# Mixing product of a two-layer kernel: from full-array products to two 64-row halves of the array

## What is computed

```python
x = x + _L0_ffn_ref(_L0_cond_ref(x, ...), L0_ffn_weight)      # grouped convolution, then an int8-style product
x = x + _L1_ffn_ref(_L1_cond_ref(x, ...), W, b, A, Bmat, LiMEs)

# _L1_cond_ref: every batch b has its own 64 x 64 weight, built from 8 kernels
agg_w = jnp.einsum('bk,koi->boi', att, weight[..., 0])
out = jnp.einsum('boi,bih->boh', agg_w, x) + agg_b[:, :, None]
```

## Time and profile before

| | before |
|---|---|
| median of 3 executions | 752.04 us (751.64 to 752.83) |
| profiled execution | 748.49 us |
| its span, first to last instruction | 746.6 us |
| mean granted TensorE clock | 0.995 |
| PE / PEld / DVE / ACT / POOL busy | 729.5 / 436.6 / 413.5 / 285.8 / 275.3 us |
| mixing product: PE busy, records | 64.1 us, 512 |
| mixing product: PEld busy, records | 59.7 us, 512 |

### The profile page before, as it was taken

One profiled execution on the slowest core, in us unless ns is written; L12 is line 12 of the kernel. 1 busy time (PEld: TensorE's weight loads), 2 busy tenths in 40 slices (PEclk: granted clock), 3 DMA queues, 4 the chain that ended last, 5 costly groups with the idle time before them and its releaser, 6 DMA issues. The chain is left out here.

```text
span 746.6 us, 10961 instructions
## 1 busy us (share of the span) xinstructions
PE 729.5 (98%) x3966; PEld 436.6 (58%) x3998; DVE 413.5 (55%) x863; ACT 285.8 (38%) x540; POOL 275.3 (37%) x158
## 2 busy tenths in 40 slices
PE   7989999999999999999999999999999999999998
PEld 6666676777777777767755444444444444444443
DVE  5756777777777877777855486523132222222233
ACT  2656887746656655555552223310111011001000
POOL 3012213213677632221245418964443443343000
PEclk9899999999999999999999999999999999999999
DMA  9579675675776565455236104533434343342102
GB/s 318 193 102 368 249 260 195 223 252 189 239 243 231 205 225 202 174 191 198 85 113 255 57 29 169 220 148 140 169 120 157 146 160 123 146 164 85 57 29 112
DMA packets 47766, 129.58 MB, mean 174 GB/s; under 512 B 16402, under 2 KB 16786, under 8 KB 47538
## 3 DMA queue, kind: packets, MB, share of 16 engines
q1 hardware_dynamic: 42962, 112.11, 43.0%
q10 hardware_dynamic: 4752, 16.78, 5.6%
HBM read 80.62 MB, written 48.25 MB: 173 GB/s over the span
## 5 line engine op out<-in xcount | busy, mean ns | idle before, releaser
L456 PE MATMUL ps<-ffn_wT,ring 128*128 128x512 f16 x1536 | 338.6, 379 | 0.0
L456 PEld LDWEIGHTS ps<-ffn_wT,ring 128*128 128x128 f16 x1536 | 149.6, 98 | 180.4 <-issue 1.3
L873 POOL TENSOR_TENSOR x<-x_in,f 128x512 f32<-128x512 f32 x64 | 74.5, 1174 | 257.4 <-DVE f L1025 257.3
L396 PE MATMUL ps<-wqT,yqT 128*128 128x512 bf16 x480 | 117.5, 380 | 1.7
L716 ACT ACTIVATE row_bias<-wsum_b,mixb_col 128x1024 f32<-128x1024 f32 x32 | 36.7, 1148 | 202.1 <-DVE mixT L1254 72.5
L693 ACT ACTIVATE yv<-yb,yinv 128x128 f32<-128x128 f32 x256 | 78.1, 388 | 12.2 <-DVE yinv L1010 11.6
L353 PE MATMUL ps<-x_ph,conv_w 128*128 128x256 f32 x256 | 79.7, 393 | 0.9 <-DMA x_ph<-in_x_phases 0.9
L354 PE MATMUL ps<-x_ph,conv_w 128*128 128x256 f32 x256 | 77.4, 384 | 0.0
L396 PEld LDWEIGHTS ps<-wqT,yqT 128*128 128x128 bf16 x512 | 47.7, 98 | 44.1
L1062 DVE SCALAR_TENSOR_TENSOR mixT<-ps,unscale,mixT 128x512 f32<-128x512 f32 x24 | 18.0, 751 | 84.1 <-PE ps L456 84.0
L383 PE MATMUL ps<-mixT,x 128*128 128x128 f32 x512 | 64.1, 278 | 0.0
(11 more groups left out here) (201 smaller groups left out, 742.1 us busy)
## 6 DMA issues: line engine op xcount, KB each, us to landing
x_ph<-in_x_phases SPq DMA_DIRECT2D x32, 516.0 KB, 5.7
x_in<-in_x SPq DMA_DIRECT2D x32, 512.0 KB, 6.1
x_scratch<-x SPq DMA_DIRECT2D x32, 512.0 KB, 2.7
x_scratch<-ring SPq DMA_DIRECT2D x26, 512.0 KB, 4.0
ring<-x_scratch SPq DMA_DIRECT2D x26, 512.0 KB, 3.2
mixT<-x_scratch SPq DMA_DIRECT2D x12, 512.0 KB, 4.1
out<-mixT ACTq DMA_DIRECT2D x12, 512.0 KB, 2.6
x_ph<-x_scratch SPq DMA_DIRECT2D x11, 512.0 KB, 4.1
```

Of the source, the lines that this page charges most:

```text
L396: last = mm(acc_bank(t, h), yqT[:, p, :], wqT[:, p, h * HALF:(h + 1) * HALF], start=p == 0, stop=p == PH - 1)
L456: last = mm(o, x2_cols[:, x2_slot(n), a, k, :], ffn_wT[:, w, k, h * HALF:(h + 1) * HALF], start=k == 0 and i == 0, stop=k == NL - 1 and i ...
L873: g.tensor_tensor(x1[:, t % 2, s], x_in[:, t % 3, s], f16[:, s], ALU.add).then_inc(sem("x1_ready"), 1)
```

## The change

`mix` becomes one call per tile. It takes each batch by itself: batch e lies on rows 64e to 64e + 63, its stationary operand is those 64 rows of a 128-position block, its moving operand the 64 columns of its own block of mixT, and its results go to bank 2 + e. So there are 16 products of 64 x 128 by 64 x 64 where there were 8 of 128 x 128 by 128 x 128, in turn on the two row halves of the array. The zero blocks of mixT are no longer read, but are still written. The call waits for both evictions of the tile before, and `mix_ready` rises by 2 at its end. A bank now holds one batch of all eight position blocks, so `high` and `low` write eight runs of 64 columns, 128 columns apart. The contents of the ring are unchanged.

```diff
-            def mix(t, h):
-                if t == 0 and h == 0:
+            def mix(t):
+                if t == 0:
                     pe.wait_ge(sem("mixT_loaded"), 64)
                 wait(pe, "x1_ready", 2 * t + 2)
-                wait(pe, "lo_ready", 2 * t - 1 + h)
-                for k in range(4):
-                    ck = 4 * h + k
-                    last = mm(ps_mix[:, ck * P:(ck + 1) * P], x1[:, t % 2, ck * P:(ck + 1) * P], mixT[:, t, :], start=True, stop=True)
-                last.then_inc(sem("mix_ready"), 1)
+                wait(pe, "lo_ready", 2 * t)
+                for k in range(NL):
+                    for e in range(2):
+                        b = slice(e * CH, (e + 1) * CH)
+                        last = mm(bank(2 + e)[:, k * CH:(k + 1) * CH], x1[b, t % 2, k * P:(k + 1) * P], mixT[b, t, b], start=True, stop=True)
+                last.then_inc(sem("mix_ready"), 2)
...
-                mix(c - 2, 0)
-                mix(c - 2, 1)
+                mix(c - 2)
...
-                A(x2_cols[:, t % RING, 0, 4 * h:4 * h + 4, :].rearrange("p c t -> p (c t)"), bank(2 + h),
+                A(x2_cols[:, t % RING, 0, :, h * CH:(h + 1) * CH], bank(2 + h).rearrange("p (c t) -> p c t", c=NL),
                   ACT.Copy, scale=t_up[:, t % 4:t % 4 + 1]).then_inc(sem("hi_ready"), 1)
...
-                v.scalar_tensor_tensor(x2_cols[:, t % RING, 1, 4 * h:4 * h + 4, :].rearrange("p k t -> p (k t)"), bank(2 + h),
-                                       t_up[:, t % 4:t % 4 + 1], x2_cols[:, t % RING, 0, 4 * h:4 * h + 4, :].rearrange("p k t -> p (k t)"),
+                cols = slice(h * CH, (h + 1) * CH)
+                v.scalar_tensor_tensor(x2_cols[:, t % RING, 1, :, cols], bank(2 + h).rearrange("p (k t) -> p k t", k=NL),
+                                       t_up[:, t % 4:t % 4 + 1], x2_cols[:, t % RING, 0, :, cols],
                                        ALU.mult, ALU.subtract).then_inc(sem("lo_ready"), 1)
```

More of the change, by code:

```diff
@@ L570, in _ @@
             tokens_out(NT - 1)
-            mix(NT - 2, 0)
-            mix(NT - 2, 1)
+            mix(NT - 2)
             dense(0, 0, 5, 8)
@@ L577, in _ @@
             row_total(NT - 1)
-            mix(NT - 1, 0)
-            mix(NT - 1, 1)
+            mix(NT - 1)
             dense(0, 1, 4, 8)
```

## The result

| | before | after |
|---|---|---|
| median, first comparison | 751.84 us (749.87 to 752.83) | 756.97 us (755.89 to 758.80) |
| ratio, 95% interval | | 1.008 (1.0054 to 1.0106) |
| profiled execution, its span | 748.49, 746.6 us | 758.80, 757.0 us |
| mean granted clock in it | 0.995 | 0.984 |

The change costs 5.1 us. The forecast was slower, 762.5 us, its likely values 754 to 769 us and its whole range 750 to 790 us. The sign and the mechanism were right, and the size of the step, 10.5 us, was twice what was measured.

A forecast was written before the change was run, and what follows sets the result against it. PE's instruction stream was taken to bound the kernel. Stage +0.12 and division changes +0.21 make 0.33 us a tile, x 32 = +10.5 on 752.04: 762.5 us, likely 754 to 769, whole range 750 to 790.

The forecast's parts named there:

- What bounds the kernel: From 64 to 400 us PE's instruction stream sets the time; a microsecond per tile in the mixing stage counts 32 times.
- Loads bind, not moving columns: Mixing stage: halving moving columns alone gives nothing; a 128-column f32 load costs 0.11 to 0.12 us whatever its rows.
- Row halves load side by side: Mixing stage: loads of both row halves overlap, 17 slots of 0.115 us, 1.96 against 1.84 us, +0.12 a tile.
- 16 slots, or 17 because the second half starts one record late: Mixing stage: slot count if halves load side by side; 17 taken, as the second half's product stands behind two records.
- The two changes of division: Entering and leaving the mixing stage between full-array work costs 0.21 us a tile together, bounds 0 to 0.33.
- The sum: Mixing stage: 0.12 + 0.21 = 0.33 us a tile, x 32 = +10.5 us, bounds +2 and +17.
- The covers: Joint wait and signal around mix cost zero: evictions end about 6 us ahead, 4 us in odd tiles.
- A: Rival, mixing stage: loads of row halves share one path, 32 slots, +71 us, 823 us; chance 0.20.
- B: Rival, mixing stage: 64-row loads take half, 0.057 us, stage 0.91 us, -23 us, 729 us; chance 0.04.
- C: Rival, mixing stage's borders: change of division is free, 16 to 17 slots of 0.107, 748 to 751 us; chance 0.10.
- D: Rival, mixing stage: the clock falls with half the moving columns; no size given, no chance of its own.

The follow-up runs named there:

- (5): The changed kernel with only the upper row half's eight products a tile, the second batch left out: 757.98 us, ratio 1.0112 to the kernel before.
- (6): The changed kernel with 64 stationary columns a product instead of 128, half of the positions left out: 740.20 us, ratio 0.9875 to the kernel before.
- (4): The changed kernel with all eight products of the upper row half ahead of all eight of the lower: 820.59 us, ratio 1.0934 to the kernel before.
- (3): The changed kernel with its 16 products a tile in two blocks of eight, full-array matmuls between them: 767.18 us, ratio 1.0217 to the kernel before.
- (2): The kernel before with its full-array products, but one joint wait and one signal a tile: 750.20 us against 751.77, ratio 0.9985.
- on quarters: The changed kernel with each product split into two of 64 stationary columns, 32 a tile: 742.06 us against 749.48 of the kernel before, ratio 0.9891.

## Why the prediction was right, and where it was off

**What bounds the kernel: right.** TensorE's stream sets the loop's time; 0.20 us on each pass arrives at the loop's end undiminished from the 10th start on.

**Loads bind, not moving columns: right, and shown.** Halving the moving columns gave nothing, a half left out saved nothing (5), and with half the stationary columns in each load the stage fell from 2.00 to 1.15 us (6).

**Row halves load side by side: right** (4, 5 and the windows). The term was off in one step: "16 slots, or 17 because the second half starts one record late". It is 16. Two loads start together at the stage's start, where one half alone starts one every 0.11 us (5), although two records of the first half stand ahead of the second's in the program. The stage costs +0.00 us, not +0.12.

**The two changes of division: right in size.** 0.20 us measured for 0.21, 0.10 on either side, and 0.19 to 0.26 more when doubled (3). It was read off one row, L439, that differed in everything but its being narrower than the array in its rows, with bounds from 0 to 0.33. That the charge is paid was understood; that it agrees to 0.01 us is partly luck.

**The sum: off by a slot that isn't paid, and by charging all 32 passes.** 0.33 x 32 = 10.5 was forecast; 0.20 us in about 24 passes, 4.8 us, came, in agreement with 5.1 us between the medians. Of the missing 5.7 us, 3.8 are the slot that isn't paid (32 x 0.12), some 1.0 the passes of the loop in which TensorE waits anyway (5 x 0.20), and 0.6 the stages of tiles 0, 1 and 31. These lie outside the count from the 3rd start to the 32nd, among the waits and clock falls of start and tail, and what they cost is not shown. The last 0.3 us is 0.21 a tile against 0.20. The waits were in the trace: L364 waits for ACT at 84.97, 106.81 and 129.59, and the stretch from 64 to 400 us has 4 us in which PE isn't busy.

**The covers: right.** The joint signal costs nothing (2), and the strided evictions take 683 and 728 ns as before. That L686 would wait for TensorE only at the tail was wrong: the eviction waits 14 times, 15.8 us, and nobody misses it.

**The rivals.** A (loads share one path) fell with experiment 5. A queue in another order comes near its total of 823 us (4), but only 44 us of that are slots. B (short loads cheaper by rows) fell: 192 ns with 64 rows. For the Trainium skill's factor of up to two, "TensorEngine Tiling (Array Packing)", Theoretical Speedup, the kernel gives 1.0 on row halves, since the time to load did not shrink; on quarters, where it does, the stage goes from 1.84 us to 16 x 0.059 = 0.94. C (a free change) fell: 0.20 us a pass. D was dismissed on rows nearly empty of columns, with the clock of 64 to 400 us beside them, but L532 lies at 49.57 us, outside that stretch, and the start, where TensorE idles shortly before, was not looked at. The result held for the changed kernel's loop (1.00 from 64 to 400 us); the reason didn't carry it, for in experiment 4, with the same columns in a longer stage, the clock of that stretch is 0.95.

## What to carry to other kernels

Before splitting the array, find which of the two streams, loads or matmuls, has the pitch. The trace can tell before anything is changed: look for a row with few moving columns. If its pitch is no shorter, the loads bind, and fewer stationary columns in each load are what helps. In this kernel row halves doubled the count of loads, hid them, and paid 0.1 us at each border with full-array work; splitting rows and columns at once nearly halved the stage. A stage that gets shorter takes cover from what follows it: ask which eviction it had been hiding. And where records are missing, read a wait from the loads and from the distance of starts, not from the list of waits alone.

## What the runs showed that had not been expected

Two halves of the array start together even where the program has two records of the first ahead of the second, but the reach of this is short: with eight products of one half ahead, 28 slots are needed for 32 loads. Four quarters run side by side in f32, 128 instructions in 1.16 us. And the time from the start to the third tile differs by 3 us between two executions of one kernel, which hides effects of 1 to 2 us placed there.
